# A fused mLSTM-attention and feed-forward kernel: z turned with the state's reading, two z tiles on ScalarE, another warm-up

## The reference

```
z  = layernorm(x)
x1 = x  + mlstm(q=z, k=ctx, v=ctx, gates from [z, ctx, ctx])
y  = x1 + ffn(layernorm(x1))
```

## Time and profile before

| | |
|---|---|
| median of 3 runs | 769.78 us (769.71 to 769.81) |
| the profiled execution's own time | 770.03 us |
| its span, first to last instruction | 768.1 us |
| PE busy | 758.7 us, 99% of the span |
| weight loads (PEld) | 632.8 us, 82% |
| DVE busy | 544.4 us, 71% |
| ACT busy | 383.2 us, 50% |
| POOL busy | 53.6 us, 7% |
| granted TensorE clock, mean | 1.000 |

### The profile page before, as it was taken

One profiled execution on the slowest core, in us unless ns is written; L12 is line 12 of the kernel. 1 busy time (PEld: TensorE's weight loads), 2 busy tenths in 40 slices (PEclk: granted clock), 3 DMA queues, 4 the chain that ended last, 5 costly groups with the idle time before them and its releaser, 6 DMA issues.

```text
span 768.1 us, 15198 instructions
## 1 busy us (share of the span) xinstructions
PE 758.7 (99%) x6296; PEld 632.8 (82%) x6296; DVE 544.4 (71%) x1296; ACT 383.2 (50%) x575; POOL 53.6 (7%) x67
## 2 busy tenths in 40 slices
PE   8999999999999999999999999999999999999998
PEld 6778888888897888878888888888889788888887
DVE  6788777586956968578675877758695693965554
ACT  3565546364455633556454554636445562435332
POOL 3400020000200011000200002000020000000000
PEclk9999999999999999999999999999999999999999
DMA  9294002301022000310005000230102100440540
GB/s 327 79 405 143 29 30 76 145 9 51 29 111 83 29 31 27 139 56 29 30 28 193 0 30 29 73 148 6 53 29 111 55 1 3 168 161 6 176 148 30
DMA packets 14617, 63.46 MB, mean 83 GB/s; under 512 B 2016, under 2 KB 2896, under 8 KB 11728
## 3 DMA queue, kind: packets, MB, share of 16 engines
q1 hardware_dynamic: 12960, 50.12, 18.9%
q0 software_dynamic: 1296, 11.53, 3.9%
q10 hardware_dynamic: 288, 0.79, 0.3%
HBM read 53.94 MB, written 8.50 MB: 81 GB/s over the span
## 4 chain that ended last, share of the span: by engine, by line
PE 84%; DVE 12%; ACT 2%; issue 1%; POOL 0%; DVEq 0%; POOLq 0%; ACTq 0%
PE ps_f L1594 24%; PE ps_f L1595 24%; DVE decay L982 8%; PE ps_f L1560 8%; PE ps_f L1561 8%; PE ps_f L1634 4%; PE ps_f L1635 4%; PE ps_a L1485 2%; PE ps_a L1502 2%; DVE decay L998 2%; PE ps_a L1337 2%; PE ps_a L1533 1%; PE ps_f L1431 1%; PE ps_f L1712 1%; PE ps_a L1373 1%
## 5 line engine op out<-in xcount | busy, mean ns | idle before, releaser
L1594 PE MATMUL ps_f<-h_hi,wgt 128*128 128x512 f32 x1024 | 401.7, 392 | 0.0
L1595 PE MATMUL ps_f<-h_lo,wgt 128*128 128x512 f32 x1024 | 398.8, 389 | 0.0
L1594 PEld LDWEIGHTS ps_f<-h_hi,wgt 128*128 128x128 f32 x1024 | 192.2, 188 | 41.6 <-issue 0.3
L1595 PEld LDWEIGHTS ps_f<-h_lo,wgt 128*128 128x128 f32 x1024 | 192.3, 188 | 38.8
L749 ACT ACTIVATE work<-ps_f,scl 128x512 f32<-128x512 f32 x128 | 87.5, 684 | 161.2 <-PE ps_f L1595 160.6
L1165 DVE TENSOR_TENSOR h_lo<-work,h_hi 128x512 fp32r<-128x512 f32 x128 | 86.5, 689 | 98.1 <-ACT h_hi L754 97.0
L1560 PE MATMUL ps_f<-h_hi,wgt 128*128 128x512 f32 x252 | 99.8, 396 | 0.0
L1561 PE MATMUL ps_f<-h_lo,wgt 128*128 128x512 f32 x252 | 98.7, 392 | 0.0
L736 ACT ACTIVATE work<-ps_f,scl 128x512 f32<-128x512 f32 x64 | 44.1, 689 | 96.8 <-PE ps_f L1561 96.3
L754 ACT ACTIVATE h_hi<-work 128x512 fp32r<-128x512 f32 x128 | 81.0, 633 | 4.1
L1156 DVE SCALAR_TENSOR_TENSOR work<-ps_f,scl,work 128x512 f32<-128x512 f32 x64 | 48.1, 751 | 45.8 <-ACT work L736 45.7
(11 more groups left out here) (216 smaller groups left out, 690.9 us busy)
## 6 DMA issues: line engine op xcount, KB each, us to landing
decay<-m_rows SPq DMA_DIRECT2D x14, 1024.0 KB, 5.9
decay<-w_cols SPq DMA_DIRECT2D x22, 512.0 KB, 4.3
wgt<-w_cols POOLq DMA_DIRECT2D x5, 1024.0 KB, 12.0
v_aug<-ctx_tok SPq DMA_DIRECT2D x8, 528.0 KB, 4.4
wgt<-w_cols POOLq DMA_DIRECT2D x2, 2048.0 KB, 13.7
x_kept<-xs SPq DMA_DIRECT2D x8, 512.0 KB, 2.6
xs<-x SPq DMA_DIRECT2D x7, 512.0 KB, 3.7
ctxT<-ctx_t SPq DMA_DIRECT2D x7, 512.0 KB, 3.7
```

The source lines that it names most:

```text
L1594: pe.matmul(ps_f[:, bank], w, moving(h_hi[layer][:, k], as_is), start=(k == 0), stop=False)
L1595: last = pe.matmul(ps_f[:, bank], w, moving(h_lo[layer][:, k], as_is), start=False, stop=(k == KH - 1))
```

## The change

- **Steady loop.** `turn_z(g)` leaves its place in layer 1 (`between_3`) and is run in layer 0, between the halves of m=7, right after `read_state(j)` and the late values. For this the banks are dealt anew: the late values go to banks 0 and 1 of `ps_a`, the turned z to banks 2 and 3, and what the state's reading gives goes for the first sequence to a bank of `ps_f` and for the second to the free columns of banks 0 and 1. `read_state` waits for the gelu that frees that `ps_f` bank; layer 1 takes its banks in the order 0, 1, 3, 2; `take_far` becomes two DVE instructions, the second of which waits for the late values.
- **Lead.** Two of the four z2 tiles (2 and 3) are centred and scaled on ACT instead of one. `first_x1_kept` is run before the gates of pair 1, not after. `keep_clock` products: 14 become 10 at the start, two wide and two narrow become one and six ahead of the scan, one wide and seven become nine ahead of the turn of z2.

```diff
-        CENTRED = Q - 1
+        CENTRED = (2, 3)
...
-            return ps_a[:, 2 + b, 0:HEADS * DV]
+            return ps_a[:, b if t else 2 + b, 0:HEADS * DV]
+
+        def zT_out(j):
+            return ps_a[:, 0:CH] if plain(j) else ps_a[:, 2:2 + CH]
+
+        FAR = CH * ROWGRP * DV
+        FAR_PART = ROWGRP * DV
+
+        def far_bank(j):
+            return (turn_of(j - 1) + 2) % 4
+
+        def hidden_bank(i, layer, m):
+            return (turn_of(i) + ((0, 1, 3, 2) if layer else (0, 1, 2, 3))[m % 4]) % 4
...
             def centre_first():
                 act.wait_ge(s_mean, 1)
-                act.activation(z2[:, CENTRED], x1_first(CENTRED), ACT.Identity, bias=minus_mean[:]).then_inc(s_centred, 1)
+                for q in CENTRED:
+                    act.activation(z2[:, q], x1_first(q), ACT.Identity, bias=minus_mean[:, q:q + 1]).then_inc(s_centred, 1)
...
             def take_far(j):
 
                 dve.wait_ge(s_farmm, j + 1)
+                if not first(j):
+                    far = state[:].rearrange("p (b h d) -> p b h d", b=W, d=DV)
+                    u = e_cols[:, 1, 1, :].rearrange("p (b h o) -> p b h o", b=W, o=1).to_broadcast([P, W, HEADS, DV])
+                    dve.tensor_tensor(far[:, 0], ps_f[:, far_bank(j), 0:FAR].rearrange("p (h d) -> p h d", d=DV), u[:, 0], ALU.mult)
+                    dve.wait_ge(s_pv, Q * j + Q)
+                    parts = ps_a[:, 0:CH, FAR:FAR + FAR_PART].rearrange("p c (h d) -> p c h d", d=DV)
+                    dve.tensor_tensor(far[:, 1].rearrange("p (c h) d -> p c h d", c=CH), parts,
+                                      u[:, 1].rearrange("p (c h) d -> p c h d", c=CH), ALU.mult).then_inc(s_far, 1)
+                    return
...
             def turn_z(j):
                 pe.wait_ge(s_z, j)
 
-                if j >= 2:
-                    pe.wait_ge(s_num, j)
-                else:
+                if plain(j):
                     pe.wait_ge(s_far, j)
-                turn(z, ps_a[:, 0:CH], s_zT)
+                turn(z, zT_out(j), s_zT)
...
             def gates(j):
...
-                pe.wait_ge(s_zTe, j + 1)
-
-                pe.wait_ge(s_num, j)
+                pe.wait_ge(s_zhi, j - W + 1)
...
             def values(j, t, b):
-                if t == 1:
-
-                    pe.wait_ge(s_near, j + 1)
...
             def read_state(j):
                 pe.wait_ge(s_state, j + 1)
+                if not first(j):
+                    pe.wait_ge(s_gelu, 2 * KH * (j - 1) + 7)
...
-                        pe.wait_ge(s_gelu, 2 * KH * i + group - 3)
+                        pe.wait_ge(s_gelu, 2 * KH * i + (group - 2 if layer == 1 and m == 2 else group - 3))
+                    if layer == 1 and m == 3 and isinstance(i, int) and i + 1 < PAIRS:
+                        pe.wait_ge(s_far, i + 2)
...
                         read_state(j)
                         values(j, 1, 0)
                         values(j, 1, 1)
+                    if g_stage and m == 7:
+                        turn_z(g)
...
                 def between_3(k):
-                    if g_stage and k == 3:
-                        turn_z(g)
+                    pass
...
             pe.wait_ge(s_ident, 5)
-            keep_clock(14, ps_f[:, 3])
+            keep_clock(10, ps_f[:, 3])
...
-            keep_clock_wide(2, ps_f[:, 3])
-            keep_clock(2, ps_f[:, 3])
+            keep_clock_wide(1, ps_f[:, 3])
+            keep_clock(6, ps_f[:, 3])
...
             turn_z(1)
+            first_x1_kept()
             plain_gates_normed(1)
-            first_x1_kept()
             first_x1_mixed()
-            keep_clock_wide(1, ps_a[:, 2])
-            keep_clock(7, ps_a[:, 2])
+            keep_clock(9, ps_a[:, 2])
```

More of the change, by code:

```diff
@@ L131, in build @@
         mv = sb("mv", [P, Q, 2])
-        minus_mean = sb("minus_mean", [P, 1])
+        minus_mean = sb("minus_mean", [P, Q])
         nw = sb("nw", [P, 4, Q])
@@ L606, in take_zT @@
             def take_zT(j):
-                source = ps_a[:, 0:CH]
+                source = zT_out(j)
                 if first(j):
@@ L715, in centre_first @@
                 act.wait_ge(s_mean, 1)
-                act.activation(z2[:, CENTRED], x1_first(CENTRED), ACT.Identity, bias=minus_mean[:]).then_inc(s_centred, 1)
+                for q in CENTRED:
+                    act.activation(z2[:, q], x1_first(q), ACT.Identity, bias=minus_mean[:, q:q + 1]).then_inc(s_centred, 1)
             def scale_first():
                 act.wait_ge(s_norm_root, 1)
-                act.wait_ge(s_centred, 1)
-                act.activation(z2[:, CENTRED], z2[:, CENTRED], ACT.Copy, scale=nw[:, 3, CENTRED:CENTRED + 1]).then_inc(s_z2_scaled, 1)
+                for n, q in enumerate(CENTRED):
+                    act.wait_ge(s_centred, n + 1)
+                    act.activation(z2[:, q], z2[:, q], ACT.Copy, scale=nw[:, 3, q:q + 1]).then_inc(s_z2_scaled, 1)
             def take_z2T(j):
@@ L748, in gelu @@
                     act.wait_ge(s_lo, n - GELU + 1)
-                act.activation(work[:, m % GELU], ps_f[:, (turn_of(i) + m) % 4], ACT.Gelu,
+                act.activation(work[:, m % GELU], ps_f[:, hidden_bank(i, layer, m)], ACT.Gelu,
                                scale=scl[:, 2 + layer, m:m + 1]).then_inc(s_gelu, 1)
@@ L1019, in take_num @@
                 dst = num[:].rearrange("p (b t e) -> p b t e", b=W, t=TILES)[:, :, 1]
-                dve.tensor_tensor(dst, ps_a[:, 2:4, 0:HEADS * DV], state[:].rearrange("p (b n) -> p b n", b=W), ALU.add)\
+                dve.tensor_tensor(dst, ps_a[:, 0:W, 0:HEADS * DV], state[:].rearrange("p (b n) -> p b n", b=W), ALU.add)\
                    .then_inc(s_num, 1)
@@ L1065, in first_norm_2_stats @@
                 dve.tensor_scalar(nw[:, 0, 0:Q], mv[:, :, 1], LN_EPS, None, ALU.add).then_inc(s_var, 1)
-                dve.tensor_scalar(minus_mean[:], mv[:, CENTRED, 0:1], -1.0, None, ALU.mult).then_inc(s_mean, 1)
+                dve.tensor_scalar(minus_mean[:], mv[:, :, 0], -1.0, None, ALU.mult).then_inc(s_mean, 1)
             def first_norm_2_apply():
@@ L1071, in first_norm_2_apply @@
                 for q in range(Q):
-                    if q != CENTRED:
+                    if q not in CENTRED:
                         dve.tensor_scalar(z2[:, q], x1_first(q), mv[:, q, 0:1], nw[:, 3, q:q + 1], ALU.subtract, ALU.mult).then_inc(s_z2_first, 1)
@@ L1415, in first_turn_z2 @@
             def first_turn_z2():
-                for q in (0, CENTRED, 1, 2):
-                    if q == CENTRED:
-                        pe.wait_ge(s_z2_scaled, 1)
+                for q in (0, 2, 1, 3):
+                    if q in CENTRED:
+                        pe.wait_ge(s_z2_scaled, CENTRED.index(q) + 1)
                     else:
@@ L1423, in first_turn_z2 @@
                         last = pe.transpose(ps_a[:, c, q * P:(q + 1) * P], z2[:, q, c * P:(c + 1) * P], ident[:])
-                        if q == 2:
+                        if q == Q - 1:
                             last.then_inc(s_z2T if c else s_z2T_first, 1)
@@ L1532, in read_state @@
                         n = ROWGRP * DV
-                        last = pe.matmul(ps_a[:, b, c * n:(c + 1) * n], zT(j)[:, c, at],
+                        if first(j):
+                            to = ps_a[:, b, c * n:(c + 1) * n]
+                        elif b == 0:
+                            to = ps_f[:, far_bank(j), c * n:(c + 1) * n]
+                        else:
+                            to = ps_a[:, c, FAR:FAR + n]
+                        last = pe.matmul(to, zT(j)[:, c, at],
                                          state[:, (b * CH + c) * n:(b * CH + c + 1) * n], start=True, stop=True)
@@ L1576, in hidden @@
                 unit = UNIT_H1 + group
-                bank = (turn_of(i) + m) % 4
+                bank = hidden_bank(i, layer, m)
                 if ks[0] == 0:
```

## The result

The changed kernel takes **778.51 us** (median of 4 runs, 777.79 to 779.38), the kernel before 769.75 us beside it (769.37 to 769.81): ratio 1.0111, 95% interval 1.01 to 1.0123. It is slower by 8.8 us. Forecast were 775.8 us and a range up to 777.9: the sign came, and so did the forecast's wait, but the median lies 0.6 us above the range. The profiled execution took 777.79 us, the shortest of the four.

The account below looks back on a forecast made before the run. PE was taken as the bound (84% of the chain of waits), with 0.90 us of slack before DVE's line 959. 770.03 - 2.0 (lead) + 8.1 (six pairs) = 776.1 profiled, 775.8 us as median; range 772.3 to 777.9.

Parts of the forecast that it names:

- the forecast's wait: Steady loop: PE waits 1.45 us for DVE's line 959 before turning the scan's rows, in each of six pairs.
- The turn's move closes GpSimd's gap, and DVE is held twice.: Steady loop: GpSimd's two subtractions run back to back and hold DVE's lines 1101 and 1102; path late by 2.18 us.
- DVE gets one instruction in, not two.: Steady loop: DVE runs only one instruction between GpSimd's two queued subtractions, so line 1102 is held to about 289.36.
- 772.7: Rival, steady loop: DVE slips two instructions in, path late by about 1.64 us, net 0.81 a pair; chance 0.13.
- 767.4: Rival, steady loop: no added hold, delay stays 0.77 us, PE waits 0.04, net -0.06 a pair; chance 0.14.
- PE saves 0.10 us a pair.: Steady loop: one change from small fp32 products back to large ones is saved, 0.10 us in each of six pairs.
- The lead gains 2.0.: Lead: fewer identity products, reordered first pair and z2 tiles on ACT gain 2.0 us, bounds 1.0 and 2.3.
- "The new waits cost nothing by themselves.": Steady loop: the gelu freeing the ps_f bank ends at 275.97, before the state's reading in the 277th us; cost nothing.
- the late clock: Rival, lead: fewer products leave PE at its lower clock longer, line 610 about 1 us later, 777.8 us; chance 0.06.
- Eight passes less, 0.205 us each.: Lead: four identity products less save eight passes of 0.205 us, 1.6 us of PE; 1.0 us goes through.

Follow-up runs that it names:

- experiment 3: The changed kernel with z turned again behind the fourth step of the state's stretch, as before, new banks and waits kept: 770.09 us, ratio 1.0004.
- (4): The changed kernel with one more wait: GpSimd's second subtraction of a pair starts only after DVE's mix, addition and square root's operand: 770.8 us, ratio 1.0015.
- experiment 5: The changed kernel with GpSimd's second subtraction of a pair replaced by a fill with zeros, which reads nothing: 769.66 us, ratio 1.0.
- experiment 10: The changed kernel with the first half of the state's reading in a bank free a tile earlier, GpSimd's second subtraction left as changed: 776.71 us, ratio 1.0088.
- experiment 1: The kernel before with every edit of the lead and none of the steady loop: 768.07 us, ratio 0.9981.
- experiment 8: The kernel with the lead's edits alone, with 12 PE instructions fewer in the lead (`keep_clock` 9 to 6): 768.93 us, ratio 0.999.
- experiment 2: The kernel before with the edits of the steady loop only, the lead as before: 780.79 us, ratio 1.0137.
- experiments 2 to 7: experiment 2, experiment 3, (4), experiment 5, experiment 6, and a seventh: the lead's edits alone plus the new wait for the gelu in `read_state`, 770.51 us.
- experiment 6: The changed kernel with 24 more PE instructions in the lead (`keep_clock` 9 to 15), shifting every later instruction: 781.6 us, ratio 1.0158.
- experiment 9: The changed kernel with GpSimd's second subtraction held back as in (4), and the state's first reading in a bank free a tile earlier: 769.34 us, ratio 0.9999.

## Why the prediction was wrong in its size

- *The turn's move closes GpSimd's gap, and DVE is held twice.* Right, and shown by taking each link away: the place (experiment 3), the closeness (4), the read (5). Line 1125 took 2.29 us (2.43 foreseen), path late 2.12 (2.18), 1.37 us a pair (1.35).
- *DVE gets one instruction in, not two.* Right in all six pairs; the rivals that stood on another order (772.7 and 767.4) did not come.
- *PE saves 0.10 us a pair.* Less: a pair takes 91.20 us in experiment 5, where nothing is held, 91.23 in the lead alone and 91.27 before. At the new place the turn takes 0.85 us instead of 0.79. A term 0.2 to 0.4 us too large in all six pairs.
- *The lead gains 2.0.* Right to the first large product (2.05). Then the first silu starts at 47.88, 0.86 us after ACT's table was loaded (45.74 + 1.28 = 47.02), though the first large product stands 2 us sooner than before; PE is 0.3 us late by it, in the lead alone too. Why ACT starts late was not tried and stays open.
- *"The new waits cost nothing by themselves."* **This step failed.** Its reasoning was that the gelu is done before PE's array comes to the reading of the state. That was true of the array. But PE takes up its instructions ahead of the array, and a wait that is released 1.9 us before a block of 256 small instructions holds them up, so that the next packet comes too late: 1.5 us in the profiled run, 1.8 between the medians of experiment 10 and the change. I priced each wait by what is late at the engine and never looked at the queue of the instructions themselves, although the page lists it. No rival had it, and the upper end of the range, 777.9, rested on the late clock.
- *The late clock.* It came, as a matter of tenths. The eight key gates took 1.90, 2.15 and 2.64 us in three profiles (experiment 1, the change, experiment 8). The windows of the profile print a granted clock of 1.00 from the first product on, but the record of it begins later, at 5.73, 7.17 and 8.16 us, and the products show the lower of the two levels (1.2 and 2.4 GHz) before: in experiment 8 the first three steps are 0.43 to 0.46 us and the last ones 0.22, in the change only the first is 0.46, in experiment 1 none. The first large product follows at 45.30, 45.38 and 45.88. Of the 2 us of that rival it cost the change 0.1, and 0.6 at most in these three; in experiment 2, whose lead is that of the kernel before, the record begins at 8.21 us instead of 7.11, and the first large product is 0.5 us late.
- *Eight passes less, 0.205 us each.* The reading was of a mean: of the 28 passes in rows 8, the first 22 stand 0.21 us apart and the last ones 0.11. The key gates start 1.1 us sooner in the change (7.81 and 6.69), not 1.6. The forecast took 1.0 of it, so the sum did not suffer.

The traces also time the failed step. They record when PE gets past a wait, and in pair 5 of the change that is at 554.85, right behind the end of the gelu:

```profile
554.12 0.69 ACT L763 ACTIVATE work<-ps_f,scl 128x512 f32<-128x512 f32 x1 [3.25 <-PE ps_f L1621]
```

The packet begins at 556.34, the block at 556.73, and PE goes on behind the break at 558.67. Seven kernels have this wait (the change and experiments 2 to 7), with two gaps each in late values. In all 14 PE is past the wait 1.88 us before the block, the packet begins 1.12 to 1.96 us after the wait, and PE goes on 2.20 to 2.62 us after the packet began. With the earlier bank (experiment 10, pair 5) PE is past the wait 4.27 us before the block, the packet begins 3.06 us before it, and there is no gap. In the five kernels whose break in pair 5 falls after product 122, the gap grows, with one pair out of order, from 0.67 to 1.19 us as the packet begins later, from 0.38 us ahead of the block to 0.09 us inside it. Why one packet begins 1.1 us after the wait and another 2.0 stays open, and so does the gap of 2.46 us in experiment 6, whose packet began 0.84 us inside a block without the new wait. That the place up to which PE has taken its instructions is what asks for the packet is my reading of these times, not a thing measured by itself.

Of both parts only the lead pays. Experiment 1's kernel is the fastest here, 768.07 us, 1.6 below the kernel before and 10.4 below the change. With both losses of the loop mended (experiment 9) the whole change ends at 769.34, no better than the kernel before.

## What to carry to other kernels

When an edit lets an engine off the critical path run its instructions back to back, look at whom the pause between them served: here DVE did its short two-input work in GpSimd's 1.77 us of idle time. Price a new wait on PE twice, once for the array and once for the stream of instructions behind it, above all ahead of some hundred products of 10 ns each. And time the halves of a change apart before pricing them as one: the half that was worth 1.6 us was hidden under one that cost 10.7.

## What the runs showed of the hardware that was not expected

PE can run dry of instructions. Blocks of 128 products of 128x33 with their loads take 1.26 us, as many instructions as lie between two breaks (1,536 for six), and 50 packets of 16 KB came for 12,592. Where a packet began within a microsecond of such a block's start, gaps of 0.18 to 1.19 us of idle PE followed in it, once 2.46, if the break lay near the block's end (after product 102 to 126); in pair 4 of the change, with a packet as late and the break after product 10, the block ran through. A packet that had begun 1.45 us ahead cost 0.2 us (experiment 8, pair 5), those 1.7 us and more ahead nothing. The gap moves product by product with instructions that are added 500 us earlier: six harmless products in the lead brought a gap here that cost 2.7 us.

And GpSimd is held as well as DVE: its subtraction took 3.38 us instead of 2.40 when DVE's two-input square of 1.23 us had started first.
